# Turning the carried row of states behind the second pair of scores instead of between the two pairs

## What is computed

```python
s = x_l[src] + x_r[dst] + e_feat
alpha = einsum('ehc,hc->eh', leaky_relu(s, 0.2), att)
amax = segment_max(alpha, dst)
ex = exp(alpha - amax[dst])
out = segment_sum(ex / denom[dst] * x_l[src], dst)
```

## Time and profile before

| | us |
|---|---|
| median of 3 runs | 3865.6 |
| lowest, highest | 3863.88, 3868.4 |
| the profiled execution | 3865.07 |
| its span, first to last instruction | 3863.6 |
| edge loop in it | about 240 to 1590 |

### The profile page before, as it was taken

One profiled execution on the slowest core, in us unless ns is written; L12 is line 12 of the kernel. 1 busy time (PEld: TensorE's weight loads), 2 busy tenths in 40 slices (PEclk: granted clock), 3 DMA queues, 4 the chain that ended last, 5 costly groups with the idle time before them and its releaser, 6 DMA issues. The chain is left out here.

```text
span 3863.6 us, 52752 instructions
## 1 busy us (share of the span) xinstructions
PE 3253.0 (84%) x14467; PEld 2621.9 (68%) x14468; DVE 1881.8 (49%) x3790; ACT 1356.0 (35%) x4612; POOL 1307.2 (34%) x1179
## 2 busy tenths in 40 slices
PE   3379999999999999624799889889989947899998
PEld 3257777777777777413677767767767746788887
DVE  5257766766766767584533634544363342011102
ACT  0026666666666656601221312312222202222222
POOL 3166655665655656222300300120030006111106
PEclk9689999999999999956899999989989958999999
DMA  6745554555555545425001100100100043333323
GB/s 233 245 133 133 130 128 125 131 128 127 131 127 128 131 124 132 80 75 158 7 1 36 28 1 13 44 7 10 47 7 1 1 143 87 107 114 123 118 94 103
DMA packets 319004, 356.61 MB, mean 92 GB/s; under 512 B 170905, under 2 KB 242429, under 8 KB 315306
## 3 DMA queue, kind: packets, MB, share of 16 engines
q0 software_dynamic: 73328, 180.19, 17.4%
q1 hardware_dynamic: 241128, 158.17, 14.8%
q10 hardware_dynamic: 4434, 16.73, 1.1%
HBM read 298.00 MB, written 55.83 MB: 92 GB/s over the span
## 5 line engine op out<-in xcount | busy, mean ns | idle before, releaser
L1230 POOL DMA_INDIRECT a_g<-xl_d,a_ix x480 | 482.1, 1004 | 309.9 <-issue 119.3
L1247 PE MATMUL a_pS<-g_xr,a_lt 128*128 x1680 | 544.2, 407 | 36.0 <-DVE a_r L1374 18.9
L1374 DVE SCALAR_TENSOR_TENSOR a_r<-a_pS,g_attx 128x528 f32<-128x528 f32 x420 | 290.7, 703 | 399.1 <-remote 275.8
L1255 PE MATMUL b_pM<-b_m,b_oh 128*112 128x281 f32 x1680 | 458.1, 413 | 28.0 <-DVE g_acc L1381 15.9
L1339 ACT ACTIVATE b_m<-a_g,c_pcx 128x64 f32<-128x64 f32 x1920 | 470.6, 333 | 1.6 <-issue 1.4
L1230 POOL DMA_INDIRECT XS<-xl_d,a_ix x360 | 360.8, 1002 | 230.2 <-issue 92.9
L1255 PEld LDWEIGHTS b_pM<-b_m,b_oh 128*112 128x112 f32 x1680 | 301.9, 183 | 142.8 <-issue 42.5
L1247 PEld LDWEIGHTS a_pS<-g_xr,a_lt 128*128 128x128 f32 x1680 | 313.7, 196 | 103.7 <-issue 49.1
L111 POOL TENSOR_TENSOR m_rstd<-m_ve,m_mhalf 125x5 f32<-125x5 f32 x44 | 51.9, 1179 | 923.3 <-DVE m_ve L101 914.7
L1339 ACT ACTIVATE b_m<-XS,c_pcx 128x64 f32<-128x64 f32 x1440 | 352.8, 333 | 1.4 <-issue 1.3
L398 PE MATMUL m_pH<-m_h,m_w 128*128 128x312 f32 (+1 forms) x1280 | 340.2, 426 | 7.7 <-DVE m_h L543 7.7
(11 more groups left out here) (350 smaller groups left out, 4488.8 us busy)
## 6 DMA issues: line engine op xcount, KB each, us to landing
a_db<-dl_d SPq DMA_DIRECT2D x212, 224.0 KB
f_w<-in_ffn_W1p SPq DMA_DIRECT2D x32, 1024.0 KB
m_w<-in_mix_W SPq DMA_DIRECT2D x8, 1024.0 KB
xg_d<-m_zero POOLq DMA_DIRECT2D x1, 8192.0 KB
f_w<-in_ffn_W2p SPq DMA_DIRECT2D x8, 1024.0 KB, 11.6
f_xg<-xg_d POOLq DMA_DIRECT2D x32, 256.0 KB, 3.8
y_d<-f_y POOLq DMA_DIRECT2D x32, 256.0 KB, 3.2
a_g<-xl_d,a_ix POOLq DMA_INDIRECT x480
```

What stands on the lines that cost most here:

```text
L1230: p.indirect_dma_start(out=gathered(t)[:, j, :], out_offset=None, in_=xl_d, in_offset=bass.IndirectOffsetOnAxis(ap=IX[:, t // BSTEPS, n:n ...
L1247: pe.matmul(o, lt[:, j, :], XRW[:, bass.ds(ws[h], 1), :].rearrange("p a d -> p (a d)"), start=True, stop=False)
L1255: ins = pe.matmul(pM[0:WN, h, 0:MW], OH[:, b, j, :], M[:, b, j, :], start=(j == 2 * h), stop=(j == 2 * h + 1))
L1374: v.scalar_tensor_tensor(out=R[:, 2 * h:2 * h + 2, :], in0=pS[0:TE, 2 * h:2 * h + 2, 0:GD], scalar=0.0, in1=attx[:, :].unsqueeze(1).broadc ...
```

## The change

In step tau 1 of each batch TensorE turns the two columns (L1273) behind `scores(1)` instead of between the pairs of scores, ahead of `sums(0)`. VectorE waits for them and copies them (L1414) behind `gate(1)` and the one-hot rows, straight ahead of the two scans that read the copy, instead of between the gates. No instruction is added or taken away.

```diff
--- before.py
+++ after.py
@@ -1267,11 +1267,6 @@
                         if tau == 0:
                             wait(pe, "a_alpha", base, t)
                             pe.transpose(pA[0:CP, 0:TE], AX_[:, par, :, :].rearrange("p h i -> p (h i)"), ident[:, :]).then_inc(s["c_turned"], 1)
-                        elif tau == 1:
-                            pe.wait_ge(s["c_rowscan"], n)
-                            for d in range(2):
-                                ins = pe.matmul(pY[0:CP, 240 + d:241 + d], ST[0:1, par, d, d:d + CP], one[:, :], start=True, stop=True)
-                            ins.then_inc(s["c_cols"], 1)
                         elif tau == 3:
                             pe.wait_ge(s["c_p"], n)
                             pe.wait_ge(s["c_cl"], n)
@@ -1281,6 +1276,11 @@
 
                         if scoring:
                             scores(1, ws)
+                        if tau == 1:
+                            pe.wait_ge(s["c_rowscan"], n)
+                            for d in range(2):
+                                ins = pe.matmul(pY[0:CP, 240 + d:241 + d], ST[0:1, par, d, d:d + CP], one[:, :], start=True, stop=True)
+                            ins.then_inc(s["c_cols"], 1)
                         if summing:
                             ts = (t - SUM) % RING
                             wait(pe, "b_weighed", base, t - SUM + 1)
@@ -1409,9 +1409,6 @@
                             v.wait_ge(s[f"c_breaks{par}"], 96 * i + (0 if odd else 96))
                             v.tensor_tensor_scan(FB[:, 0, :], BR[:, par, 0, :], scores, LOW, ALU.add, ALU.max)
                             v.tensor_tensor_scan(FB[:, 1, ::-1], BR[:, par, 1, ::-1], scores[:, ::-1], LOW, ALU.add, ALU.max).then_inc(s["c_scan"], 1)
-                        elif tau == 1:
-                            v.wait_ge(s["c_cols"], n)
-                            v.tensor_copy(IN[:, :], pY[0:CP, 240:242]).then_inc(s["c_init"], 1)
                         elif tau == 2:
                             v.wait_ge(s["c_max"], n)
                             v.tensor_tensor(FB[:, 1, :], scores, FB[:, 0, :], ALU.subtract).then_inc(s["c_diff"], 1)
@@ -1425,6 +1422,8 @@
                             v.tensor_tensor(OH[:, t % 2, :, :], nodes[:, :].unsqueeze(1).broadcast_to([TE, IG, WN]),
                                             DLX[:, four(base, t - WEIGH)].unsqueeze(2).broadcast_to([TE, IG, WN]), ALU.is_equal).then_inc(s["b_onehot"], 1)
                         if tau == 1:
+                            v.wait_ge(s["c_cols"], n)
+                            v.tensor_copy(IN[:, :], pY[0:CP, 240:242]).then_inc(s["c_init"], 1)
                             v.wait_ge(s["c_init"], n)
                             v.sem_inc(s["c_seen"], 1)
                             v.tensor_tensor_scan(FB[:, 0, :], BR[:, par, 0, :], scores, IN[:, 0:1], ALU.add, ALU.max)
```

## The result

The changed kernel takes 3844.69 us (median of nine runs, 3843.14 to 3854.05) against 3863.88 us (nine runs, 3851.58 to 3868.4): ratio 0.9957, 95% interval 0.9945 to 0.9969, a gain of some 17 to 19 us where 45 were forecast. The profiled execution lasts 3849.64 us, 15.4 less than that of before.

The account below looks back on a forecast made before the run. TensorE bounds the edge loop, where waiting costs about 95 us idle plus 50 us of low clock. Gross 69.7 us, capped at 48 net by GpSimd's rhythm, taken as 45: 3865.1 - 45 = 3820 us, range 3780 to 3860.

Parts of the forecast that it names:

- The replay: Batch 14's step 1 recomputed in the new order with its own rows: 6.85 us instead of 11.86.
- the gross of 69.7 us: Steps 1 that wait for the columns: 18 x (10.72 - 6.85) = 69.7 us gained before any give-back.
- The rule weighed from the Trainium skill: TensorE in step 1: short idle spells between matmul groups can make the clock swing; then only 32 us would come.
- VectorE's part at 0 us: VectorE's moved copy, 0.14 us, 30 times, costs 0 us, covered by idling before its gates.
- the 12 us that a lost cover was put at: VectorE's moved copy: cost if idling before the gates no longer hid it, 30 x (0.14 + 0.27) = 12 us.
- GpSimd's rhythm as the bound of the give-back: Edge loop: gather bursts and pauses keep a batch from going under 44.1 us, capping the net gain at 48 us.
- the other bound: Second give-back bound: nine batches not waiting at the columns average 45.46 us, giving 24 us net.
- Case 5: Late notice settles on step 6's second scores; transpose waits, clock drops, batch 47.62 us; 3880 if all 18; chance 0.08.
- Case 3: Most is given back by other batches' waits (24 us, 3841), or clock stays low (32 us, 3833); chance 0.14.
- Case 2: No give-back, gathers' rhythm stretches: 3795 us, or 3783 with VectorE also ahead; chance 0.20.
- case 4: Wait moves with the columns to before the sums, or the same 5 us return at step 0's transpose: 3865; chance 0.08.
- cases 1 and 5: Case 1 is the forecast itself: 3820 us (3800 to 3835), give-back near the gathers' rhythm; chance 0.50.

Follow-up runs that it names:

- e1: Kernel before, with the gathers left out of all rounds but the first, on the first chip: 3719.30 us, 144 less than before.
- e4: Changed kernel with VectorE's copy and its wait put back between the gates, so only TensorE's order changes: 3844.58 us, ratio 0.9957.
- e5: Changed kernel with transpose behind second scores, row of states behind second sums, VectorE's step-0 scans left between the gates; second chip: 3704.65 us, ratio 1.0002.
- e11: Changed kernel with transpose behind second scores, row of states behind second sums, scans between the gates, on the third chip: 3705.21 us, ratio 1.0001.
- e13: Changed kernel with transpose behind second scores, row of states behind second sums, scans between the gates, on the fourth chip: 3705.93 us, ratio 0.9999.
- e17: Changed kernel with transpose behind second scores, row of states behind second sums, scans between the gates, on the fifth chip: 3706.64 us, ratio 1.0003.
- e3: Changed kernel with transpose behind second scores, VectorE's step-0 scans behind the one-hot rows, row of states behind second sums; first chip: 3890.35 us, ratio 1.0067.
- e10: The changed kernel, unchanged, on the third chip, without late notices: 3704.05 us, ratio 0.9997 to before.
- e9: The kernel before, unchanged, run for its trace on the third chip, without late notices: 3704.09 us.

## Why the prediction was right and wrong

**What bounds the kernel: right, for the chips that it is true of.** The 95 us of idle TensorE and 50 us of low clock that I read as all that waiting can cost in the loop are, to within 1 us, what e1 gave back: 144 us.

**Step 1: right for each step, by luck near in the sum.** The replay said 6.85 us where the late notice falls, at clock 1.00. Measured: 6.89 to 7.02 in those, 6.13 in the rest, all at 1.00. But the replay took all 18 to keep their late notice, and only eight have one now. Eighteen at about 6.95 would have given 18 x (10.72 - 6.95) = 68 us; the gross of 69.7 us came as 74.5 because notices went from step 1 to other steps. The prediction put the idling before the second scores and the columns at "about 0.5 and 0.35"; in the profile's idle times it is 0.33 to 0.46 and 0.1. The rule weighed from the Trainium skill ("TensorE: Matmul & The Clock Gate", section "A second HAM failure mode: psum-queue depth-cycling") did not bite where I asked it: two idle spells of under 0.5 us in each of these eight steps left the clock up. The clock fell in steps 0 instead, in nine of the twelve with a wait before the transpose, after 3.4 to 3.7 us from start to start; two waits of 2.3 and 2.7 us and one of 3.5 us left it at 1.00.

**VectorE's part at 0 us: right.** e4, without it, is as fast (0.9957 both). e4 does not price the 12 us that a lost cover was put at, since the cover was there.

**GpSimd's rhythm as the bound of the give-back: near the mean of the good batches, no floor, and wrong as a forecast.** The floor was 6 gathers in 9.45 us, 44.1 us a batch. The fifteen batches without a wait at the transpose last 44.53 in the mean, but seven of them lie below the floor, between 43.28 and 44.0 us; two already did in the trace of before (44.02, and the 43.36 of the earlier trace rows). The twelve others last 47.17. 12 x 47.17 + 15 x 44.53 over 27 is 45.70.

**The step that failed** is the choice inside the give-back: "I take 45, near the rhythm's bound, because that mean holds the batch of 47.62 with its 3.10 us wait, which needs one particular place of the late notice." I took the other bound, 24 us from the nine batches that don't wait at the columns (45.46 a batch), for a pessimistic one, and it was the better estimate: 45.5 to 45.7 was measured. The place wasn't rare. In batches 2 to 28 of the trace of before, gaps over 0.6 us before the transpose, from start to start, are there in 9 batches and sum to 20.8 us; in that of after in 12, with 40.0 us, ten of them between 3.4 and 3.7 us. What was mis-sized is the give-back: 69.7 - 45 = 25 us were forecast, 74.5 - 19.8 = 55 were measured, 28.9 of them in steps 0. The argument that it needs one place of the notice was true of a single batch, and was no measure of how often the notice would take it once the columns no longer caught it first.

**The rivals.** Case 5 named the mechanism (the notice settles on the last scores of step 6, the transpose waits, the clock drops, the batch lasts about 47.6) and the point from which it decides, 0.82 of the batches. It came in 12 of 27, 0.44, at 47.17 a batch. Against the fifteen others that is 12 x (47.17 - 44.53) = 32 us, the largest part of what was given back, and less than half of the gross gain. Case 3, 24 us net, is the nearest sum. Case 2 did not come in the mean (45.70 a batch, where it needed 42.9), though single batches do go under 44.1. Of case 4 the first half is out, as no wait stands before the columns or the sums behind them; its second half, the same 5 us at the transpose of step 0, is what the twelve batches show (134.34/12 = 11.2 us a step 0, where one without a wait takes 6.49), but not in all. What I had missed is that cases 1 and 5 aren't alternatives for the whole loop but for each batch; weighing 47.6 and 44.1 at, say, half each gives 45.85 a batch, a net gain of 18 x (46.77 - 45.85) = 17 us. The half is chosen with the result known; nothing that I had read before gave it.

**What stays open.** What makes the notices late on one chip and not on four others isn't known, nor whether it is the chip at all or the hour, since each chip ran in one stretch of time. Only leaving out all gathers was tried where they are late (e1). Half the gathers, thinner ones, a shorter lead and the transpose behind the second scores with the scans left in place (e5, e11, e13, e17) ran only where nothing is late. Whether that last one would gain on a chip like the first isn't known; e3, its nearest form there, lost 0.7%. Nor are the 24.0 us in steps 2 and 4 explained. No kernel here beats both on either kind of chip.

## What to carry to other kernels

A wait taken away from one place in a loop is caught by the next piece that needs the same late result; count the places where it can be caught, price a cycle for each, and mix them, before booking the gain. Here an instruction that waits for another engine's newest result cost less behind work that had long been ready: 0.4% gained where results come late, nothing lost where they don't (e10). The next such move, made together with its producer's, lost 0.7% (e3). Ask of a wait with an unnamed releaser whether it belongs to the kernel at all: a second chip may not show it.

## What the hardware showed that I had not expected

The same kernel takes 3863 us on one chip and 3704 to 3706 us on four others, 4% apart, one stretch of time on each, with medians within 0.1% of each other among those four. The whole difference lies in the edge loop: 46.03 against 40.87 us a batch. On the first chip VectorE waits up to 4.9 us for matmuls that have ended (93 waits, 262.2 us). It isn't alone: GpSimd and ScalarE, which wait for TensorE too, have such waits in the trace of before, while TensorE, which waits for VectorE and ScalarE, has none:

```profile
POOL a_g L1230 <- remote: 112.0, 59, 2.8
...
ACT b_m L1335 <- remote: 87.1, 20, 7.2
```

SyncE's loads have them as well, where they wait for TensorE (82.6 us in 22 places and 62.0 us in 10), while SyncE's waits for VectorE have a named releaser and come to 163.9 us in before and 163.8 in e9. In e9's trace no engine has a wait for an unnamed releaser in the loop. So what is late is what TensorE signals, to every engine that waits for it, and not VectorE's start as such. Without gathers the same chip keeps the pace of the others (40.99). Why is not shown by any run here.

On the chips without late notices GpSimd, busy for about two thirds of the edge loop (783 of 1210 us), couldn't take on 0.58 us more a step without the kernel losing 0.67 us a step.
